# One vector addition of a graph-network kernel written as a reduction over pairs

## The reference, cut to what matters

```python
proj = einsum('ni,rio->nro', x, relation_weight)
att  = sum(proj[src, etype] * tanh(proj[dst, etype] + edge_attr), -1)
a    = softmax of att over the edges of each destination
h_nb = segment_sum(x[src] * a[:, None], dst)
out  = leaky_relu((x + h_nb) @ res_fc_w.T, 0.01) + leaky_relu((x * h_nb) @ res_fc2_w.T, 0.01)
result = layernorm(x + out)          # no scale, no shift, eps 1e-5
```

## Time and profile before

| what | value |
|---|---|
| median of three runs | 761.22 us |
| the profiled execution's own time | 762.27 us |
| its span, first to last instruction | 760.5 us |
| mean granted TensorE clock | 0.921 of full |
| busy: PE, DVE, ACT, POOL | 76%, 79%, 67%, 76% of the span |

### The profile page before, as it was taken

The page is one execution under the profiler, slowest core; times in us unless marked ns, Lnnn a source line. Parts: engine busy times, 40 slices in busy tenths (PEclk is TensorE's granted clock), DMA queues, the critical chain, the costliest instruction groups (busy, mean ns, idle before and its releaser), DMA issues. The chain is left out here.

```text
span 760.5 us, 13886 instructions
## 1 busy us (share of the span) xinstructions
PE 574.4 (76%) x3948; PEld 313.6 (41%) x3948; DVE 603.9 (79%) x1094; ACT 507.9 (67%) x1457; POOL 575.6 (76%) x594
## 2 busy tenths in 40 slices
PE   1897988888898898798898797898888988650000
PEld 0643454444454454454454453444444444450000
DVE  2589899999999999999999999899888888750010
ACT  0376877779879878878878879656655556770040
POOL 6777777777777777777777777777777777777776
PEclk9999999999999999999999999999999999855555
DMA  4643443343353343354343243321222210000000
GB/s 115 177 123 91 137 152 114 97 151 85 108 165 107 94 155 92 113 151 109 93 155 108 67 124 97 105 67 48 75 75 73 68 48 33 32 25 18 19 18 16
DMA packets 48034, 70.37 MB, mean 93 GB/s; under 512 B 15970, under 2 KB 19486, under 8 KB 47958
## 3 DMA queue, kind: packets, MB, share of 16 engines
q1 hardware_dynamic: 18562, 32.97, 13.8%
q0 software_dynamic: 18752, 17.29, 10.5%
q10 hardware_dynamic: 10644, 19.23, 6.8%
HBM read 45.60 MB, written 25.78 MB: 94 GB/s over the span
## 5 line engine op out<-in xcount | busy, mean ns | idle before, releaser
L450 POOL DMA_INDIRECT xsd<-in_x,ends_i x388 | 380.8, 982 | 119.9 <-issue 107.7
L999 DVE SCALAR_TENSOR_TENSOR xm<-typ,xT_ps 128x1024 f32<-128x1024 f32 (+1 forms) x225 | 264.2, 1184 | 3.0 <-ACT xc L719 2.6
L558 PE MATMUL t_ps<-xm,w_rel 64*64 64x512 f32 (+1 forms) x900 | 241.5, 617 | 13.7 <-DVE xm L999 11.0
L560 PE MATMUL h_ps<-xm,w_rel 64*64 64x512 f32 (+1 forms) x900 | 241.4, 617 | 0.0
L474 POOL DMA_INDIRECT out<-out_r,row_i x196 | 191.7, 978 | 59.7 <-issue 57.0
L578 PE MATMUL y_ps<-bd_cat,dT 128*128 128x256 f32 x392 | 98.4, 395 | 11.3 <-DVE zd L1061 5.4
L743 ACT ACTIVATE o_t<-zd,rstd 128x64 f32<-128x64 f32 x392 | 98.8, 339 | 6.3 <-DVE rstd L1083 6.3
L558 PEld LDWEIGHTS t_ps<-xm,w_rel 64*64 64x64 f32 x900 | 46.9, 133 | 105.2 <-DVE xm L999 76.8
L578 PEld LDWEIGHTS y_ps<-bd_cat,dT 128*128 128x128 f32 x392 | 72.7, 196 | 25.1 <-ACT dT L724 11.0
L588 PE MATMUL tr_ps<-ident,uw 128*128 128x128 f32 x196 | 33.5, 297 | 44.5 <-ACT uwT L788 24.0
L1041 DVE SCALAR_TENSOR_TENSOR es<-es,wd,wx 128x64 f32<-128x64 f32 x196 | 55.2, 282 | 11.2 <-DVE es L1041 0.5
(11 more groups left out here) (161 smaller groups left out, 957.9 us busy)
## 6 DMA issues: line engine op xcount, KB each, us to landing
x_in<-in_x SPq DMA_DIRECT2D x48, 256.0 KB, 2.7
typ<-typ_d SPq DMA_DIRECT2D x24, 512.0 KB
out<-o_t ACTq DMA_DIRECT2D x48, 256.0 KB
xsd<-in_x SPq DMA_DIRECT2D x512, 0.2 KB
xsd<-in_x,ends_i POOLq DMA_INDIRECT x388, 2.7
hist<-es ACTq DMA_DIRECT2D x24, 256.0 KB, 2.7
ea<-in_edge_attr SPq DMA_DIRECT2D x24, 224.0 KB
out<-out_r,row_i POOLq DMA_INDIRECT x196, 2.1
```

The lines of the kernel that those rows point to most:

```text
L450: pool.indirect_dma_start(xsd[:, s % RX, j, side, :], None, x[:, :], bass.IndirectOffsetOnAxis(ap=ends_i[:, side, c:c + 1], axis=0),).then ...
L558: pe.matmul(t_ps[h * D:(h + 1) * D, 0:n], w[0:D, :], moving[0:D, h * n:(h + 1) * n], start=(at == 0), stop=(at == R - 1), skip_group_check ...
L560: mm = pe.matmul(h_ps[(1 - h) * D:(2 - h) * D, 0:n], w[D:P, :], moving[D:P, (1 - h) * n:(2 - h) * n], start=False, stop=(at == R - 1), ski ...
L999: v.scalar_tensor_tensor(xm[:, m % RM, 0:n], typ[:, s % RT, 0:n], float(r), xT_ps[:, 0:n], ALU.is_equal, ALU.mult).then_inc(masked, 1)
```

## The change

The addition of the two parts of l12 becomes a `tensor_reduce` over them. The same tile is read with the parts as the innermost dimension: for each of the 512 sums the engine reads two elements that lie 64 elements (256 bytes) apart, 1,024 in all. The output tile, its shape, the waits and the signal stay as they are, and the place in the program too.

```diff
             def final_add(f):
                 n = cols(f)
                 v.wait_ge(l_done, f + 1)
-                v.tensor_tensor(zf[:, 0:n, :], l12[:, 0:n, 0, :], l12[:, 0:n, 1, :], ALU.add).then_inc(z1_done, 1)
+                v.tensor_reduce(zf[:, 0:n, :], l12[:, 0:n, :, :].rearrange("p j k f -> p j f k"), AX.X, ALU.add).then_inc(z1_done, 1)
```

## The result

| | before | after |
|---|---|---|
| median (22 runs each) | 761.72 us | 764.74 us |
| lowest to highest | 760.38 to 765.5 | 763.36 to 766.84 |
| the profiled execution, its span | 762.27, 760.5 us | 765.52, 763.8 us |
| mean granted TensorE clock | 0.921 | 0.921 |

The ratio is 1.0032, 95% interval 1.0021 to 1.0043, or +2.4 us. The means lie 2.5 us apart (762.28 and 764.77) and the medians 3.0: the times of the kernel before fall in two groups, eleven from 760.4 to 761.4 us and eleven from 762.0 to 765.5, and their median lies between the two. With 22 runs a difference of 0.3% can be told.

What follows compares the result with a forecast made beforehand. POOL's back-to-back transfers were taken as the bound. DVE's 1.5 + 1.0 us delay passes to POOL in step as +2.5 us, the pace adding nothing: 764.8 against the profiled execution, 764 against the median, range 760.5 to 770.

Steps and rivals of the forecast that it cites:

- The bound: Whole kernel: the time is the sum of POOL's gathers and scatters with their issue time, 584 x (0.98 + 0.30) = 748 us.
- The reduction takes 1.20 us: Line 1104: the 1,024-element reduction takes 1.20 us against the addition's 0.69, +0.51 each, 7.1 us in all.
- the sum: The forecast's addition of terms: 0.51 us per reduction, 2.5 us passed on by DVE and through POOL, 762.27 + 2.5 = 764.8.
- the estimate of about 1.9 us: Slow-read rival at line 1104: hopping reads make the reduction about 1.9 us, total 763 to 768; slow-read chance 0.20.
- What DVE passes on: DVE before the gather at 454.24: 0.51 us in each of steps 2 to 4, about 0.1 in ten later ones, 2.5 us.
- the cover: Steps 5 to 14: DVE's 3.3 us of waits ahead of line 1006 hide 0.41 of each 0.51 us.
- The pace: POOL's transfers waiting for PE instruction counts: at least 4.0 us to spare at each point, so the delay costs nothing.
- marks: PE instruction counts that each POOL transfer waits for; gather 387 asks for 5,400, with 10.9 us to spare.
- POOL in step with DVE: Gathers starting inside lines 1099 and 1092 end 0.82 us after them, so POOL takes on DVE's lateness: +2.5 us.
- the holds: Gathers starting inside a two-input DVE instruction wait until it ends, taking 1.2 to 1.65 us instead of 0.94.
- The picture: At lines 1099 and 1092, POOL starts the same gather inside the same instruction and leaves later by DVE's delay.
- the 14th addition: The last of the 14 replaced additions, behind the last held gather at 454.24; claimed to be worth nothing more.

Runs made afterwards that it cites:

- `forms`: Own kernel: POOL gathers while DVE runs blocks of one instruction form each; pairs 256 bytes apart took 1,211 ns, adjacent pairs 1,197.
- `pace`: The changed kernel with LEAD 1,400 in place of 250, so no PE mark can hold POOL; ratio 1.003 (1.0015 to 1.0045) against the kernel before.
- `delay`: The kernel before, addition kept, plus one 464-element reduction behind it in each of the 14 steps; ratio 1.0034 (1.0018 to 1.0049), +2.6 us.
- `cycles`: Own kernel: POOL gathers while DVE cycles one two-input instruction and lengthening reductions; time per gather 1.35, 1.40, 1.46, 1.27, 1.32, 1.37 us over six stages.
- `late`: The kernel before with two 640-element reductions in each of steps 17 to 23, where DVE waits anyway; ratio 0.9998 (0.998 to 1.0015).

## Why the prediction was right

- **The bound.** Right: POOL's transfers are back to back in both kernels, from 3.5 us after the start to 3.5 us before the end, so all of the 3.3 us between the spans comes from its transfers and the waits ahead of them. DVE's last instruction ends 29 us before the end. A small misreading: POOL's waits of 0.60 and 0.70 us in the kernel before were not issue time under another label; 0.7 us of them were real.
- **The reduction takes 1.20 us.** 1,240 ns, so 0.55 more than the addition, where the sum had 0.51. The Trainium skill, Vector Engine (DVE) Microarchitecture Reference, Measured stream behaviour on trn2, has the rule of a port that slows down on hops, from which the estimate of about 1.9 us came; it did not apply. The same section of the Trainium skill has the exception, one read stream alternating between two regions 16 KiB apart at the full rate. The case here, with 256 bytes, behaves like it: 14 ns over adjacent pairs (`forms`). That same reduction takes 1,211 ns alone and 1,240 in the kernel; 11 ns of the difference the old addition had as well (692 against 681 for line 1109). The rest stays open.
- **What DVE passes on**, 3 x 0.51 + 10 x 0.1 = 2.5 us. Measured 2.51 us, partly by luck: the steps 2 to 4 became 0.52 to 0.62 us longer and the others, compared at the same granted clock, 0.12 to 0.16, which makes 1.7 + 1.4 = 3.1 us; one fall of the clock fewer gives 0.45 back, which was not in my sum. The wait ahead of line 1006 was the cover: its 3.3 us are gone.
- **The pace costs nothing.** Right: no wait over 0.3 us, and `pace` without marks is as slow.
- **POOL in step with DVE, +2.5 us.** The gathers' busy time rose by 2.6 us, 6 ns each as forecast, through the holds: those by line 1099 are 1.3 us longer in all, and those by the pair of lines 1092 and 1093 1.1 us. `delay` gives the same time without the changed line. `cycles` shows by itself that the held gather takes on all of DVE's delay.
- **The picture was simpler than the case.** I had POOL start the same gather inside the same instruction, only later. In the two profiled executions DVE's first full step begins at different times (52.24 and 54.09 us), line 1092 of step 15 is only 0.65 us later than before, and POOL arrives there with one gather fewer. Of the 1.9 us by which gather 350 is late, 1.25 is that gather and 0.65 the later instruction. The profile of `late`, where DVE starts at 52.24 as after the change, is the cleaner partner: there line 1092 of step 15 starts at 452.36, so DVE is 2.28 us later after the change, and POOL, again with one gather fewer, 3.5 us; later holds give 0.3 back. So POOL did not just take on DVE's delay, it also lost a gather's place in the cycle, and that the gathers' sum came out at 2.6 us is in part luck of which two executions are compared (against `late` it is 3.3).
- **What I left out.** I called the 14th addition worth nothing, since the last hold of a gather lies ahead of it. The scatters are held too, by line 1136: four in the kernel before, seven after, and they account for most of 1.4 us between the two profiles. It is not just one execution against another. The two profiles whose DVE is on time up to step 16 have 191.7 us of scatters, the kernel before and `late`; the three with a DVE that is late have 193.1 (the change), and in `pace` and `delay`:

```profile
L474 POOL DMA_INDIRECT out<-out_r,row_i x196 | 192.8, 984 | 59.7 <-issue 56.6
...
L475 POOL DMA_INDIRECT out<-out_r,row_i x196 | 192.8, 983 | 59.7 <-issue 57.0
```

So 1.1 to 1.4 us of scatters come with the lateness, a term that the sum had at nothing. That the total still fits is luck as well: the profiles are 3.3 us apart, the means of 22 runs 2.5 and the medians 3.0, and the forecast had 2.5.

No run of a kernel that computes the reference was measurably faster than the kernel before where that takes 762 us. The holds, 15.5 us in the kernel before, are what there is to gain on POOL; taking them away while still computing the slope, the products and the centring was not tried.

## What to carry to other kernels

Where an engine that issues indirect transfers is back to back, its instructions are the time, and the busy share of the others says little. Look at its longer instructions, at what ran beside them when they started, and whether the one ends a fixed time after the other; if so, the two are in step, and a delay of the engine that seems to have slack passes through whole until one more transfer fits in (shown in `cycles`; in the kernel itself only the delay of half a microsecond was measured). A reduction over pairs costs by what it reads, not by what it writes (1,024 elements take 1.20 us whether 16, 512 or 1,024 come out), so it is no replacement for an addition of two tiles. Its one merit is that it holds no gather, and the old addition held none here.

## What the hardware showed that I had not expected

- A DVE instruction with a broadcast column and a tile in SBUF (line 79 of `forms`, 48 of them without a break) kept POOL out for 29.5 us, until 0.82 us after the last. The other two forms with two SBUF inputs let POOL in between two instructions.
- A held gather ends 0.81 to 0.83 us after the end of the DVE instruction, a held scatter 0.84 to 0.85 us.
- DVE gives way as well. Beside POOL in step with it, every second addition of line 64 took 723 ns in place of 676.
- In the two kernels of my own, where POOL's gathers need no register or wait between them, every 28th was preceded by 2.3 us of issue time. In the kernel of this case no such gap is seen. Its cause is open.
- The kernel before took 760 to 765.5 us on some chips and 903 to 933 us on three others, in all of 63 runs of it there. The profiles there show waits of up to 4.9 us for issue on PE. I did not look for the cause.
